# A tenth product on GpSimd in every chunk of a selective scan, and an earlier request for the rows of B

## The chip, the cores and the metric

The kernel runs on one core of a Trainium2 chip, as one program from the first load to the last store. The metric is the device time of that core in microseconds (us), the median of several executions. Below, TensorE is PE, VectorE is DVE, ScalarE is ACT, GpSimd is POOL and SyncE is SP.

## What is computed

Four layers, one after the other, each a vision block built on a selective scan over images of 64 x 64 tokens (8 images, 96 channels, doubled to 192 inside). Three layers scan in four directions, the last in one. Cut to what matters, a direction does this for every channel d and each of 16 states n:

```
delta = softplus(dts + bias)                    # per channel and token
def step(h, inp):
    u_t, d_t, b_t, c_t = inp
    dA = jnp.exp(d_t[..., None] * A[None])
    h = dA * h + (d_t * u_t)[..., None] * b_t[:, :, None, :]
    y = jnp.einsum('bkdn,bkn->bkd', h, c_t)
    return (h, y)
```

The product of delta*u (in the kernel: du) and B feeds the recurrence, and the product of h and C is summed over the 16 states. Around the scan stand projections, a depthwise convolution, a norm and a gate, which the change doesn't touch.

## The kernel before

Each layer is three stages: `expand_stage`, `scan_stage` and `merge_stage`. The change is in `scan_stage` alone. It works on chunks of 1024 tokens of a pair of images in one direction; 208 chunks in all (64 in each of the first three layers, 16 in the last). A loop body holds two chunks (`BODY_CHUNKS`), so there are 104 bodies, and all orders are written out by hand inside a body.

A chunk has three tiles of channels (`TILES`) with 16 states each: 48 **steps**. Two steps make a **unit**, so a chunk has 24 units, eight to a tile (`TILE_UNITS`), and a body 48. In this text units are counted 0 to 23 in a chunk; the tiles are units 0 to 7, 8 to 15 and 16 to 23. Four units (a quad) share one copy of delta and of du, `delta4_` (three buffers) and `du4_` (two buffers), spread over the partitions by DMA.

What happens to a unit depends on where its product du*B is made:

- In most units PE copies the rows of B over the partitions into PSUM (`slot`, L899), ACT makes the decay exp(delta*A) into `decay` (L1102), DVE multiplies du with the slot, one instruction a step (L1037), and DVE scans, one instruction a step (L1063).
- In the units named by `POOL_UNITS`, 2, 5 and 7 of each tile, nine in a chunk, POOL makes the product for both steps in one instruction of 128 x 2048 elements into `made` (L1284), from `du4_` and from rows of B that a DMA has spread into `b4_` (two buffers, `B_RING`). ACT puts the decay into the slot, and DVE only scans (L1059).

Behind the scans of every unit POOL multiplies h with C for both steps (`gate`, L1263), and PE sums over the states (`reduce`, L969). POOL also makes du = delta*u once a tile (L1276). POOL's order, in each unit v: at v = 4 of a tile the du of the next tile; then, if unit v + 2 is one of POOL's (`POOL_LEAD` is 2), its product; then the gate of v, which waits for the scans of v.

SP issues all the DMAs from one queue, in order, and waits in that queue. For each unit v, `after_gate` does this, in this order: in units 8 to 11 of each half chunk of 12, the rows of C for four units later (`load_c`, four DMAs); if v is one of POOL's units, the rows of B for the product two further on (`load_b`, four DMAs); in unit 4 of a tile the first quad of du of the next tile (`spread_du`, eight DMAs); in unit 7 its second quad; in unit 3 the first quad of delta of the next tile (`spread_delta`, eight DMAs); in unit 4 its second quad. Ahead of rows of C, rows of B, and the second quad of du, SP waits on `gated` until the gate of v is done (L807); ahead of the others it waits for `du_ready` (L814) or `delta_ready` (L820). The order in unit 4 of the last tile, where all three fall together, is thus: rows of C, du, delta.

On DVE, the first multiply of a quad waits until all eight DMAs of its du have landed (`du_in`, L1034), and both scans of a POOL unit wait for `pool_multiplied` (L1058). Each new quad of du overwrites the quad before the last.

Of the kernel before, what the change touches and what calls it, by code (L numbers as in the profile page):

```python
# [31 lines left out]
TILES = 3  # L32
# [20 lines left out]
QUADS, GROUP = 4, 32  # L53
UNITS = STEPS // 2
TILE_UNITS = UNITS // TILES
PAIRS_OF_GROUPS = UNITS // QUADS
BATCH_UNITS = UNITS // 2


POOL_UNITS, POOL_LEAD = (2, 5, 7), 2  # L60
H_RING, DECAY_RING, DELTA_RING, DU_RING, B_RING, MADE_RING = 4, 3, 3, 2, 2, 2
AHEAD, FILL_LAG, REDUCE_LAG = 2, 2, 2
FLAT = 2 * NS * CH // P
# [10 lines left out]
DU_AT, Y_STORE = 4, 1  # L74
# [523 lines left out]
def scan_stage(nc, kind, T, W, useq, neg_a, yseq, bcdram, splitdram):  # L598
# [18 lines left out]
    BU = BODY_CHUNKS * UNITS  # L617
    BODY_PAIRS = BODY_CHUNKS * PAIRS_OF_GROUPS


    on_pool = [v for v in range(BU) if v % TILE_UNITS in POOL_UNITS]
    PB = len(on_pool)
    assert PB % B_RING == 0 and PB % MADE_RING == 0 and BU % H_RING == 0 and BODY_PAIRS % DELTA_RING == 0 and BODY_PAIRS % DU_RING == 0

    def place(s):
# [7 lines left out]
    def pair_of(v):  # L633

        return v // QUADS
# [20 lines left out]
    C_BODY = 64 * 2 * BODY_CHUNKS  # L656
    B_BODY = 64 * PB // B_RING
    DELTA_BODY = 128 * BODY_PAIRS // DELTA_RING
# [8 lines left out]
    with ExitStack() as ctx:  # L667
# [52 lines left out]
        with nc.Block() as block:  # L720
            @block.sync
            def _(sp):
# [34 lines left out]
                def load_quad(dst, signal, v, base):  # L757


                    q = v // UNITS % BODY_CHUNKS  # L760
                    for j in range(QUADS):
                        row = base + NS * batch_of(v) + QUADS * (v % QUADS) + j
                        sp.dma_start(dst[GROUP * j:GROUP * j + GROUP, :],
                                     bcdram[q, row:row + 1, :].broadcast_to((GROUP, CH))).then_inc(signal, 16)

                def load_c(v):
                    load_quad(c4[v % QUADS], c_in[v % QUADS], v, 2 * NS)

                def load_b(k):
                    load_quad(b4[k % B_RING], b_in[k % B_RING], on_pool[k % PB] + BU * (k // PB), 0)  # L770

# [10 lines left out]
                def spread_delta(j):  # L782
                    spread_pair(delta4[j % DELTA_RING], delta_in[j % DELTA_RING], delta[:, 1:], j)

                def spread_du(j):
                    spread_pair(du4[j % DU_RING], du_in[j % DU_RING], du, j, 1)

                def store_y(i, C0, T_):

                    q, t = T_ // TILES, T_ % TILES  # L790
                    sp.wait_ge(sem["y_copied"], C0 * TILES + (T_ + 2))
                    here = chunk_and_direction(i, q)[0]
                    if backward(q):
                        here = here + SEQS[kind] * PAIRS * NCH
                    sp.dma_start(yseq[here, t], ybuf[:]).then_inc(sem["y_stored"], 16)

                def after_gate(i, C0, v):

                    if v % TILE_UNITS == Y_STORE and v >= TILE_UNITS:
                        store_y(i, C0, v // TILE_UNITS - 1)  # L800
                    if v >= BU:
                        return
                    n, T_ = v % TILE_UNITS, v // TILE_UNITS
                    new_c, new_b = v % BATCH_UNITS >= BATCH_UNITS - QUADS, v in on_pool
                    if new_c or new_b or n == DU_OUT_AT[1]:

                        sp.wait_ge(sem["gated"], C0 * UNITS + (v + 1 + REDUCE_LAG))  # L807
                    if new_c:
                        load_c(v + QUADS)
                    if new_b:  # L810
                        load_b(on_pool.index(v) + B_RING)
                    if n == DU_OUT_AT[0]:

                        sp.wait_ge(sem["du_ready"], C0 * TILES + (T_ + 2))  # L814
                        spread_du(2 * T_ + 2)
                    if n == DU_OUT_AT[1]:
                        spread_du(2 * T_ + 3)
                    if n == DELTA_OUT_AT[0]:

                        sp.wait_ge(sem["delta_ready"], C0 * TILES + (T_ + 2))  # L820
                        spread_delta(2 * T_ + 2)
                    if n == DELTA_OUT_AT[1]:
                        spread_delta(2 * T_ + 3)
# [36 lines left out]
                for v in range(Y_STORE + 1):  # L860
                    after_gate(0, 0, v)
                with sp.Fori(0, NC // BODY_CHUNKS) as i:
                    C0 = i * BODY_CHUNKS
                    for v in range(Y_STORE + 1, BU + Y_STORE + 1):
                        after_gate(i, C0, v)
                        if v < BU:
                            chunk_work(i, C0, v)
# [158 lines left out]
            def _(dve):  # L1026
# [13 lines left out]
                def scan(C0, body, s, g):  # L1040
# [15 lines left out]
                    if v in on_pool:  # L1056
                        p = on_pool.index(v)
                        dve.wait_ge(sem["pool_multiplied"], body * PB + (p + 1))  # L1058
                        dve.tensor_tensor_scan(out, slot[s % 2][:, order], made[p % MADE_RING][:, s % 2, order],  # L1059
# [193 lines left out]
            def _(pool):  # L1253
# [24 lines left out]
                def multiply(i, v):  # L1278

                    k = on_pool.index(v % BU) + PB * (v // BU)  # L1280
                    j = pair_of(v)
# [397 lines left out]
def build(nc, args, out, layers=(0, 1, 2, 3)):  # L1679
# [12 lines left out]
    with ExitStack() as ctx:  # L1692
# [25 lines left out]
        for n in layers:  # L1718
            kind = KINDS[n]
            count = SEQS[kind] * PAIRS * NCH  # L1720
            results = DIRS[kind] * PAIRS * NCH
            expand_stage(nc, kind, T, W[n], x_t, useq[0:count], zgate)
            scan_stage(nc, kind, T, W[n], useq[0:count], neg_a[n], yseq[0:results], bcdram, splitdram)
            merge_stage(nc, kind, T, W[n], useq[0:count], yseq[0:results], zgate, x_t, out, n == layers[-1])
# [110 lines left out]
```

## Time and profile before

| | us |
|---|---|
| median of 3 runs | 36543.74 (36541.12 to 36548.06) |
| the profiled execution | 36523.66 |
| its span | 36521.8 |
| DVE busy | 33315.6 |
| POOL busy | 31312.7 |
| PE busy | 26890.5 |
| ACT busy | 18989.0 |

The profiled execution lies 20 us below the median, and only 1.9 us lie outside its span. The span is made of four scan stages, where all of this change happens, and of the stages around them. The busy times are of the whole span, so they mix stages with different limits: a scan stage has to be read by itself. In the rows below, a row of the timeline gives the start of an instruction (or of several in a row, then with the time of all of them), its time, the engine, the line, what is written and read, the count, and in brackets the idle time of the engine before it and what ended it. Queue rows of SP (SPq) show the time that SP took to issue the DMAs, not when they landed.

### The profile page before, as it was taken

Reading aid. Unit: us, or ns where it says so; the run is one execution under the profiler, and the core shown is the slowest. Engines: PE = TensorE matmul, PEld = TensorE weight load, DVE = VectorE, ACT = ScalarE, POOL = GpSimd, SP = SyncE. Lnnn points to the kernel's source line nnn. Section 1 sums busy time; section 2 is a strip of 40 time slices with the busy share of each in tenths; the row PEclk is TensorE's granted clock in tenths of the full one; section 3 lists DMA queues with packets and bytes.
Section 4 is the critical chain, followed back from the end, with each engine's and each line's share of the span. In section 5 each row is a group of like instructions: output and inputs, shape, how many; then the busy total and the mean of one; then the engine's idle time right before and its main releaser. Section 6 shows DMA issues by size and latency. Waiting matters only on the chain. (4 is left out here: it accounts for less than half of the span.)

```text
span 36521.8 us, 335475 instructions
## 1 busy us (share of the span) xinstructions
PE 26890.5 (74%) x76784; PEld 7510.4 (21%) x76784; DVE 33315.6 (91%) x18007; ACT 18989.0 (52%) x23286; POOL 31312.7 (86%) x7984
## 2 busy tenths in 40 slices
PE   5777777777766777777777766777777777766777
PEld 2111111111122111111111112111111111112114
DVE  6999999999977999999999977999999999976993
ACT  4555555555534555555555534555555555534551
POOL 1999999999962999999999961999999999974993
PEclk7888888888878888888888878888888888877885
DMA  4666666666675666666666675666666666676665
GB/s 154 172 174 173 174 174 173 173 171 174 173 237 175 173 172 174 172 173 173 172 171 173 172 233 173 174 171 173 173 174 172 172 173 172 172 240 183 174 174 178
DMA packets 2428244, 6486.11 MB, mean 178 GB/s; under 512 B 704848, under 2 KB 849616, under 8 KB 2416336
## 3 DMA queue, kind: packets, MB, share of 16 engines
q1 hardware_dynamic: 2426576, 6471.86, 66.8%
q14 instruction: 1597, 13.08, 0.1%
q8 instruction: 71, 1.16, 0.0%
HBM read 3070.92 MB, written 764.47 MB: 105 GB/s over the span
## 5 line engine op out<-in xcount | busy, mean ns | idle before, releaser
L1263 POOL TENSOR_TENSOR h<-h,c 128x2048 f32<-128x2048 f32 x4992 | 20775.3, 4178 | 571.6 <-DVE h L1063 423.3
L1063 DVE TENSOR_TENSOR_SCAN h<-decay,state,slot 128x1024 f32<-128x1024 f32 x6240 | 14647.7, 2347 | 832.8 <-issue 44.8
L969 PE MATMUL psy<-h,t_fold 128*32 128x512 f32 x40000 | 11405.6, 749 | 0.0
L899 PE MATMUL slot<-bc,pick 96*128 96x512 bf16 x12496 | 4654.1, 461 | 7571.8 <-DVE h L1059 5930.6
L1059 DVE TENSOR_TENSOR_SCAN h<-slot,state,made 128x1024 f32<-128x1024 f32 x3744 | 8565.8, 2327 | 8.8 <-ACT slot L1102 8.8
L1284 POOL TENSOR_TENSOR made<-du,b 128x2048 f32<-128x2048 f32 x1872 | 7804.1, 4169 | 723.6 <-DMA b<-bcdram 723.6
L1102 ACT ACTIVATE decay<-delta,na 128x1024 f32<-128x1024 f32 x6248 | 7066.8, 1145 | 1706.0 <-DVE h L1063 1519.0
L1037 DVE TENSOR_TENSOR slot<-du,slot 128x1024 f32<-128x1024 f32 x6240 | 7534.5, 1207 | 281.6 <-PE slot L899 254.8
L1102 ACT ACTIVATE slot<-delta,na 128x1024 f32<-128x1024 f32 x3744 | 4177.0, 1116 | 4262.3 <-DVE h L1063 4255.1
L969 PEld LDWEIGHTS psy<-h,t_fold 128*32 128x32 f32 x40000 | 2290.1, 130 | 8286.4 <-issue 7772.2
L899 PEld LDWEIGHTS slot<-bc,pick 96*128 96x128 bf16 x12496 | 776.8, 102 | 13297.0 <-DVE h L1059 9058.9
L1276 POOL TENSOR_TENSOR du<-delta,u 128x1024 f32<-128x1024 f32 x628 | 1473.0, 2346 | 2356.1 <-ACT delta L1156 2356.1
L1110 ACT COPY state<-h 128x2 f32<-128x2 f32 x4992 | 924.1, 185 | 3934.9 <-DVE h L1063 2979.0
L917 PE MATMUL psc<-dts,wdt 32*128 32x512 f32 x2512 | 1921.1, 853 | 0.9 <-ACT dts L1190 0.9
L1654 POOL TENSOR_TENSOR ya<-ya,yb 128x1024 f32<-128x1024 f32 x360 | 997.5, 2779 | 849.8 <-DMA ub<-useq 783.8
L907 PE MATMUL psc<-u,wx 128*96 128x512 f32 x2544 | 1551.8, 728 | 6.7 <-DMA bdt<-in_bdt 6.2
L1125 ACT ACTIVATE relu<-psc,bdt 128x1024 f32<-128x1024 f32 x628 | 699.8, 1114 | 1561.9 <-PE psc L917 1561.9
L1156 ACT COPY delta<-psc 128x1024 f32<-128x1024 f32 x628 | 637.2, 1015 | 1428.5 <-PE psc L936 1428.5
L1598 DVE SCALAR_TENSOR_TENSOR total<-ub,dsum,ya 128x1024 f32<-128x1024 f32 x240 | 464.7, 1943 | 899.7 <-DMA ub<-useq 514.1
L936 PE MATMUL psc<-log,t_ident 128*128 128x512 f32 x2512 | 1220.6, 608 | 8.9 <-ACT log L1139 0.2
L936 PE MATMUL psc<-relu,t_ident 128*128 128x512 f32 x2512 | 1215.1, 607 | 9.2 <-ACT ex L1126 9.2
L936 PE MATMUL psc<-excess,t_less 128*128 128x512 f32 x2512 | 1181.9, 592 | 0.0
(111 smaller groups left out, 19226.2 us busy)
## 6 DMA issues: line engine op xcount, KB each, us to landing
delta<-delta SPq DMA_DIRECT2D x10048, 128.0 KB, 2.6
du<-du SPq DMA_DIRECT2D x10048, 128.0 KB, 2.9
b<-bcdram SPq DMA_DIRECT2D x7520, 128.0 KB, 2.9
c<-bcdram SPq DMA_DIRECT2D x6720, 128.0 KB, 2.9
u<-useq SPq DMA_DIRECT2D x212, 1536.0 KB, 6.7
yseq<-ybuf SPq DMA_DIRECT2D x624, 512.0 KB, 3.0
ya<-yseq SPq DMA_DIRECT2D x420, 512.0 KB, 4.4
yb<-yseq SPq DMA_DIRECT2D x360, 512.0 KB, 5.3
```

The lines of the kernel that those rows point to most:

```text
L899: mm = pe.matmul(slot[s % 2][:, cols], pick[:, rows_of, :], bc[q % 2][:, cols], start=True, stop=True)
L907: mm = pe.matmul(psc[0:96, HALF[a]], wx[q][:, s, :], u[q][:, s, HALF[a]], start=(s == 0), stop=(s == TILES - 1))
L917: pe.matmul(psc[:, HALF[a]], wdt[q][:, t, :], dts[q][:, HALF[a]], start=True, stop=True)\
L936: mm = pe.matmul(psc[:, HALF[a]], T["less" if term == 2 else "ident"][:, :], (relu, log, excess, ex)[term][:, HALF[a]], start=(term == 0), ...
L969: mm = pe.matmul(psy[rows, cols], T["fold"][:, :], h[v % H_RING][:, c, cols], start=(v % QUADS == 0), stop=(v % QUADS == QUADS - 1), skip_ ...
L1037: dve.tensor_tensor(slot[s % 2][:], du4[j % DU_RING][:, s % 2, 1:], slot[s % 2][:], ALU.mult)\
L1059: dve.tensor_tensor_scan(out, slot[s % 2][:, order], made[p % MADE_RING][:, s % 2, order], first, ALU.mult, ALU.add).then_inc(sem["h_ready ...
L1063: dve.tensor_tensor_scan(out, decay[s % DECAY_RING][:, order], slot[s % 2][:, order], first, ALU.mult, ALU.add).then_inc(sem["h_ready"], 1)
L1102: act.activation(dst[:], delta4[j % DELTA_RING][:, s % 2, :], ACT.Exp, scale=na[q][:, k:k + 1])\
L1263: pool.tensor_tensor(both[:, :, 0:CH], both[:, :, 1:], c4[g][:, order].unsqueeze(1).broadcast_to((P, 2, CH)), ALU.mult)\
L1276: pool.tensor_tensor(du[:], delta[:, 1:], u[q][:, t, :], ALU.mult).then_inc(sem["du_ready"], 1)
L1284: pool.tensor_tensor(made[k % MADE_RING][:], du4[j % DU_RING][:, :, 1:], b4[k % B_RING][:].unsqueeze(1).broadcast_to((P, 2, CH)), ALU.mult)\
```

## The change

`POOL_UNITS` gets an entry for each of the three tiles: in the third tile of a chunk POOL makes the products of units 1, 3, 5 and 7 in place of 2, 5 and 7 (in the chunk: 17, 19, 21, 23 in place of 18, 21, 23). That is ten products a chunk, and DVE has 14 units with multiplies in place of 15. And SP asks for rows of B not at the place of the unit v whose product used the buffer, but at v - 2, where that product is made (but at unit 2 at the earliest, in the body's first tile). So in its queue SP meets B in units 3 and 5 of a tile where it met it in 5 and 7, and in the last tile in 1, 3, 5 and, for the next chunk's first product, at its unit 0.

```
-POOL_UNITS, POOL_LEAD = (2, 5, 7), 2
+POOL_UNITS, POOL_LEAD = ((2, 5, 7), (2, 5, 7), (1, 3, 5, 7)), 2
...
-    on_pool = [v for v in range(BU) if v % TILE_UNITS in POOL_UNITS]
+    on_pool = [v for v in range(BU) if v % TILE_UNITS in POOL_UNITS[v // TILE_UNITS % TILES]]
     PB = len(on_pool)
+
+    product_made = [max(v - POOL_LEAD, Y_STORE + 1) for v in on_pool]
...
-                    new_c, new_b = v % BATCH_UNITS >= BATCH_UNITS - QUADS, v in on_pool
+                    new_c, new_b = v % BATCH_UNITS >= BATCH_UNITS - QUADS, v in product_made
                     if new_c or new_b or n == DU_OUT_AT[1]:
+
 
                         sp.wait_ge(sem["gated"], C0 * UNITS + (v + 1 + REDUCE_LAG))
...
                     if new_b:
-                        load_b(on_pool.index(v) + B_RING)
+                        load_b(product_made.index(v) + B_RING)
```

POOL's instructions in the third tile of the body's first chunk, from the product made ahead of the gate of unit 15 on. `made` is a product, `h` with `c4` a gate (h3 is unit 15, h0 unit 16, h1 unit 17, h2 unit 18). Before:

```order
L1263 TENSOR_TENSOR h2_0<-h2_0,c4_2_0 128x2x1024
L1257 REGISTER_ALU
L1263 TENSOR_TENSOR h3_0<-h3_0,c4_3_0 128x2x1024
L1282 REGISTER_ALU
L1283 REGISTER_ALU
L1284 TENSOR_TENSOR made0_0<-du4_0_0,b4_0_0 128x2048
L1257 REGISTER_ALU
L1263 TENSOR_TENSOR h0_0<-h0_0,c4_0_0 128x2x1024
```

Now:

```order
L1266 TENSOR_TENSOR h2_0<-h2_0,c4_2_0 128x2x1024
L1285 REGISTER_ALU
L1286 REGISTER_ALU
L1287 TENSOR_TENSOR made0_0<-du4_0_0,b4_0_0 128x2048
L1260 REGISTER_ALU
L1266 TENSOR_TENSOR h3_0<-h3_0,c4_3_0 128x2x1024
L1260 REGISTER_ALU
L1266 TENSOR_TENSOR h0_0<-h0_0,c4_0_0 128x2x1024
L1287 TENSOR_TENSOR made1_0<-du4_0_0,b4_1_0 128x2048
L1260 REGISTER_ALU
```

The product of the tile's first POOL unit (17, not 18) now stands ahead of the gate of 15, and a further one (of 19) ahead of the gate of 17.

SP's queue in the third tile, units 18 to 20 before (from the wait for the gate of unit 18 to the second quad of delta):

```order
L807 REGISTER_ALU
L763 DMA b4_0_0<-bcdram 32x1024 [waits gated]
L763 DMA b4_0_0<-bcdram 32x1024 x3
L820 REGISTER_ALU
L778 DMA delta4_0_0<-delta_0 32x1024 [waits delta_ready]
L778 DMA delta4_0_0<-delta_0 32x1024 x7
L807 REGISTER_ALU
L763 DMA c4_0_0<-bcdram 32x1024 [waits gated]
L763 DMA c4_0_0<-bcdram 32x1024 x3
L778 DMA du4_0_0<-du_0 32x1024 [waits du_ready]
L778 DMA du4_0_0<-du_0 32x1024 x7
L778 DMA delta4_1_0<-delta_0 32x1024 x8
```

Now, units 19 and 20 (the wait for the gate of unit 19 is the first row):

```order
L810 REGISTER_ALU
L765 DMA b4_0_0<-bcdram 32x1024 [waits gated]
L765 DMA b4_0_0<-bcdram 32x1024 x3
L823 REGISTER_ALU
L780 DMA delta4_0_0<-delta_0 32x1024 [waits delta_ready]
L780 DMA delta4_0_0<-delta_0 32x1024 x7
L810 REGISTER_ALU
L765 DMA c4_0_0<-bcdram 32x1024 [waits gated]
L765 DMA c4_0_0<-bcdram 32x1024 x3
L780 DMA du4_0_0<-du_0 32x1024 [waits du_ready]
L780 DMA du4_0_0<-du_0 32x1024 x7
L780 DMA delta4_1_0<-delta_0 32x1024 x8
```

The rows read alike, but the `gated` of the rows of B just ahead of the delta is that of unit 18 before, and of unit 19 now.

## Rows read from the trace of the kernel before

**Rows 1.** The page: the costliest groups of the scan, whole program

```profile
L1263 POOL TENSOR_TENSOR h<-h,c 128x2048 f32<-128x2048 f32 x4992 | 20775.3, 4178 | 571.6 <-DVE h L1063 423.3
L1063 DVE TENSOR_TENSOR_SCAN h<-decay,state,slot 128x1024 f32<-128x1024 f32 x6240 | 14647.7, 2347 | 832.8 <-issue 44.8
...
L1059 DVE TENSOR_TENSOR_SCAN h<-slot,state,made 128x1024 f32<-128x1024 f32 x3744 | 8565.8, 2327 | 8.8 <-ACT slot L1102 8.8
L1284 POOL TENSOR_TENSOR made<-du,b 128x2048 f32<-128x2048 f32 x1872 | 7804.1, 4169 | 723.6 <-DMA b<-bcdram 723.6
...
L1037 DVE TENSOR_TENSOR slot<-du,slot 128x1024 f32<-128x1024 f32 x6240 | 7534.5, 1207 | 281.6 <-PE slot L899 254.8
```

**Rows 2.** Busy time by stretch: the four scan stages

```profile
core 0: us, PE busy (x) PEld busy (x) DVE busy (x) ACT busy (x) POOL busy (x), PEclk, DMA share, GB/s
814.00:10321.00 9507.00, 7244.08 (x20998) 1858.67 (x20994) 9243.23 (x4985) 5289.80 (x6596) 9166.82 (x2302) 0.83 0.68 173
11747.00:21285.00 9538.00, 7262.22 (x20996) 1862.62 (x20992) 9243.49 (x4985) 5290.32 (x6596) 9167.54 (x2302) 0.82 0.68 172
```

**Rows 3.** By stretch: one body; and unit 10 of its second chunk to the next body

```profile
5855.33:6151.53 296.20, 224.31 (x658) 57.92 (x656) 289.12 (x156) 165.40 (x206) 286.26 (x73) 0.83 0.69 173
6070.37:6150.20 79.83, 56.71 (x173) 14.30 (x172) 77.92 (x43) 42.94 (x54) 78.20 (x20) 0.82 0.63 159
```

**Rows 4.** Timeline of DVE: units 10, 18, start of 19, 23, next unit 0

```profile
6065.75 4.62 DVE L1059 TENSOR_TENSOR_SCAN h<-slot,state,made 128x1024 f32<-128x1024 f32 x2
...
6115.14 4.57 DVE L1059 TENSOR_TENSOR_SCAN h<-slot,state,made 128x1024 f32<-128x1024 f32 x2
6119.63 1.21 DVE L1037 TENSOR_TENSOR slot<-du,slot 128x1024 f32<-128x1024 f32 x1
...
6126.81 1.21 DVE L1037 TENSOR_TENSOR slot<-du,slot 128x1024 f32<-128x1024 f32 x1
...
6145.65 4.57 DVE L1059 TENSOR_TENSOR_SCAN h<-slot,state,made 128x1024 f32<-128x1024 f32 x2
6150.20 1.23 DVE L1037 TENSOR_TENSOR slot<-du,slot 128x1024 f32<-128x1024 f32 x1
```

**Rows 5.** Timeline of POOL from the gate of unit 10 to the next body's first product

```profile
6070.44 4.18 POOL L1263 TENSOR_TENSOR h<-h,c 128x2048 f32<-128x2048 f32 x1 [0.36 <-DVE h L1059]
6074.57 4.17 POOL L1284 TENSOR_TENSOR made<-du,b 128x2048 f32<-128x2048 f32 x1
6078.70 4.18 POOL L1263 TENSOR_TENSOR h<-h,c 128x2048 f32<-128x2048 f32 x1
6082.84 2.33 POOL L1276 TENSOR_TENSOR du<-delta,u 128x1024 f32<-128x1024 f32 x1
6085.14 4.16 POOL L1263 TENSOR_TENSOR h<-h,c 128x2048 f32<-128x2048 f32 x1
...
6115.31 4.18 POOL L1263 TENSOR_TENSOR h<-h,c 128x2048 f32<-128x2048 f32 x1 [1.26 <-DVE h L1063]
6119.79 4.18 POOL L1263 TENSOR_TENSOR h<-h,c 128x2048 f32<-128x2048 f32 x1 [0.30 <-DVE h L1059]
...
6158.30 4.17 POOL L1284 TENSOR_TENSOR made<-du,b 128x2048 f32<-128x2048 f32 x1 [3.13 <-DMA b<-bcdram]
```

**Rows 6.** Timeline of SP's queue in units 11 to 13 and 18 to 21

```profile
6094.77 5.25 SPq L778 DMA_DIRECT2D delta<-delta  x8
6100.14 1.90 SPq L763 DMA_DIRECT2D b<-bcdram  x4
...
6123.99 1.70 SPq L763 DMA_DIRECT2D b<-bcdram  x4
6130.35 4.96 SPq L778 DMA_DIRECT2D delta<-delta  x8
6138.69 1.71 SPq L763 DMA_DIRECT2D c<-bcdram  x4
6140.44 4.97 SPq L778 DMA_DIRECT2D du<-du  x8
6145.45 5.11 SPq L778 DMA_DIRECT2D delta<-delta  x8
```

**Rows 7.** DMAs of du: the eight of that group; then all 96 of about a body

```profile
L778 SPq DMA_DIRECT2D du<-du x8: 513/592/602, 6140.4 to 6144.8; - x8
...
DMA to landing us min/median/max: 2.8/3.0/3.2
```

```profile
L778 SPq DMA_DIRECT2D du<-du x96: 512/592/1144, 6011.9 to 6293.3; - x96
...
DMA to landing us min/median/max: 2.4/3.0/4.9
```

**Rows 8.** DVE's scans by line: scan stages of the first, second and third layer

```profile
L1063 DVE TENSOR_TENSOR_SCAN h<-decay,state,slot 128x1024 f32<-128x1024 f32 x1917 | 4499.9, 2347 | 238.5 <-ACT state L1207 13.1
...
L1063 DVE TENSOR_TENSOR_SCAN h<-decay,state,slot 128x1024 f32<-128x1024 f32 x1917 | 4499.9, 2347 | 270.8 <-issue 44.8 <-ACT decay L1102 3.1
...
L1063 DVE TENSOR_TENSOR_SCAN h<-decay,state,slot 128x1024 f32<-128x1024 f32 x1917 | 4499.9, 2347 | 260.3 <-DVE slot L1037 22.9 <-ACT state L1207 12.5 <-ACT decay L1102 6.9
```

**Rows 9.** Timeline of DVE where a body begins, in the second layer

```profile
14119.40 1.23 DVE L1037 TENSOR_TENSOR slot<-du,slot 128x1024 f32<-128x1024 f32 x1 [0.78 <-issue]
14121.84 2.35 DVE L1063 TENSOR_TENSOR_SCAN h<-decay,state,slot 128x1024 f32<-128x1024 f32 x1 [1.21 <-issue]
```

## Prediction

> **What bounds the kernel now.** First I read the costliest groups of the page [rows 1], then the busy time of each scan stage by itself [rows 2], then one body and one stretch of it [rows 3], and only then the timelines. The reader should see in [rows 2] that a stage of 9507 us has DVE busy for 9243 us and POOL for 9167: over 96% both. The rest of DVE's time is mostly the gap of about 0.1 us between two instructions, so in the scan DVE practically never waits. Its rhythm stands in the timeline [rows 4]: a unit whose product POOL makes takes 4.49 us (6115.14 to 6119.63), a unit with its own multiplies 7.18 us (6119.63 to 6126.81). A body of 18 and 30 such units is 18 x 4.49 + 30 x 7.18 = 296.2 us, and the body that I read takes 296.20 [rows 3]. POOL, in contrast, still waits a little: for scans (1.26, 0.36 and 0.30 us [rows 5]), and for rows of B (3.13 us in [rows 5], 723.6 us in the whole program [rows 1]). So DVE sets the time, and POOL is some 2% behind it.
>
> **Part one: the earlier request for B.** It takes away the wait of 723.6 us [rows 1]. I cost it at nothing by itself: the wait is POOL's, at the first product of a chunk, and DVE runs through those same units without a wait (a body lasts exactly the sum of its units [rows 3]). Shifted alone it would give back POOL time that nobody needs. Its price is in SP's queue: in the last tile the request now stands in unit 19, behind a wait for that unit's gate and ahead of the delta and du spreads of the next tile.
>
> **Part two: the tenth product.** DVE loses one unit's two multiplies: 7.18 - 4.49 = 2.69 us a chunk, 208 x 2.69 = 560 us if nothing else came late. POOL gains one product of 4.13 us (6074.57 to 6078.70, start to start [rows 5]). Per chunk DVE would need 10 x 4.49 + 14 x 7.18 = 145.4 us and POOL 24 + 10 operations of 4.13 and three du of 2.30 (6082.84 to 6085.14), 147.3 us, against 148.1 us of DVE now. So of 560 us at most 208 x (148.1 - 147.3) = 166 us can be had, and only if POOL never waits.
>
> It will wait, because the extra load is all in the last tile. I take one stretch of the timeline [rows 3 to 5]: in unit 10 POOL has caught up (its gate starts 0.07 us behind the scans, 6065.75 + 4.62 = 6070.37 against 6070.44), and in the new order nothing ahead of that point is heavier, so it will have caught up there again. The measure is the time from the end of the scans of unit 10 to the first multiply of the next chunk: now 6150.20 - 6070.37 = 79.83 us, all of it DVE's own work. In the new order three chains run over the same stretch:
>
> - DVE itself: 79.83 - 2.69 = 77.1 us.
> - POOL's last product (unit 23), which DVE needs. From the gate of unit 10 on POOL has 11 gates, 6 products and 2 du ahead of its end: 0.07 + 17 x 4.13 + 2 x 2.30 + 0.05 (an operation lasts about 0.05 us beyond the next one's start) = 74.9 us. With 0.08 us to wake DVE and 4.57 us for the two scans of unit 23 [rows 4] the next chunk starts at 79.6 us. So the saving on DVE is used up by a wait for that product, to within 79.83 - 79.6 = 0.2 us.
> - The du of the next chunk's first quad, through SP. The gate of unit 19 ends after 10 gates, 5 products and 1 du: 0.07 + 15 x 4.13 + 2.30 + 0.05 = 64.4 us. Only then may SP issue B (1.70 us, at 6123.99 in [rows 6]), the delta (4.96), C (1.90, as a group of four took directly behind delta at 6100.14) and du. With the small gaps between them (0.03, 0.10, 0.12 and 0.04) the du group begins at 73.2 us. Its last DMA is issued 4.4 us later (6140.4 to 6144.8 [rows 7]) and lands after 2.8 us (the lowest of that group; the median is 3.0): 80.4 us, and with 0.07 us to wake DVE **80.5 us**. The wait for gate 20 ahead of C is no limit, since that gate ends at 64.4 + 2.30 + 4.13 = 70.8 us and SP arrives at 71.2.
>
> Before, du was early: its last DMA was issued at 6144.8 and landed at about 6147.6, 2.6 us ahead of the multiply. Now both its cover (the slack) and the 2.69 us of DVE work that stood over it are gone. The third chain ends last, so a chunk lasts 80.5 - 79.8 = 0.7 us longer than now, not 2.69 less: 208 x 0.67 = +139 us.
>
> **What is hidden in it.** DVE pauses where a new body begins: in the second layer before the first multiply and the first scan, with nothing that the profile could name [rows 9], 44.8 us in its 32 bodies [rows 8]. In the first and third layer the rows name 13.1, 22.9 and 12.5 us more. Together that is 93 us. A wait for du in front of the first multiply runs at the same time as such a pause. I take 74 us of it, about four fifths, as hidden under the new wait (bounds: 0 and 93). Sum: +139 - 74 = **+65 us**. In the profiled execution's terms that is 36523.66 + 65 = 36589, and on the median 36543.74 + 65 = 36609.
>
> The other tiles are no trouble: in units 3 and 11 POOL is only 1 to 2 us behind, so du is issued some 5 us earlier relative to DVE. PE and ACT have work for 76% and 56% of a body [rows 3] and lose the fills of two units a body. Operations of POOL and DVE keep their times: the products take 4.17 us while DVE is busy all the time, so more of them add no new kind of neighbour.
>
> **What the Trainium skill says to it.** A product takes 4.17 us [rows 5], the two multiplies that it replaces 2 x 1.207 = 2.41 us [rows 1]. The Trainium skill, "GPSIMD Engine Reference", sections 3.1 and 4.1, speaks against the change: two-input elementwise work belongs on VectorE, and a float32 tensor_tensor of 2048 elements takes 4497 ns on GpSimd. With that figure for the six products the second chain would end 6 x 0.33 = 2.0 us later, an estimate of about +1.7 us a chunk; the trace has the duration, and decides for 4.17.
>
> The landing of a du DMA takes 2.8 to 3.2 us [rows 7]. The Trainium skill, "DMA: Bandwidth & Descriptors", section "Anatomy of one DMA", gives 2.0 us plus the bytes at 436 GB/s (for the path through GpSimd): for 128 KB an estimate of 2.3 us. By that du would land 0.5 us earlier and the sum would be 0.5 x 208 = 104 us lower; the rows of the trace don't support it.
>
> **The rivals.**
>
> - **Du lands in time, the product alone sets the pace.** It happens if SP gets through its four groups 0.9 us faster. A chunk takes 79.6 us over the stretch: -0.28 x 208 = -58 us, 36486. For it: the groups have been seen a little shorter. Against: it takes the lowest figures for all four at once.
> - **POOL never waits.** If POOL comes into each chunk late enough to be busy throughout, its 147.3 us set the period: -166 us, 36378. Against it: the first 11 units of a chunk hold four POOL units in the new order as before, and there POOL catches up today.
> - **The du chain is longer: slower.** Landings of up to 4.9 us are seen [rows 7]. The queue now carries four groups back to back. If the last du lands 1 us later than I take, that is another +208 us (36817); at 4.9 us, 2.1 us later, +437 us (37046). It decides from a landing of 2.84 us on that the kernel is slower by over 0.2%. For it: after long runs of C and B groups landings grow. Against: delta groups, issued at a slower pace, stand between them, and the du group that follows a C group [rows 6] still landed in 2.8 to 3.2 us.
> - **The change doesn't do what it says:** a wait for B stays, because SP comes late to the earlier place. It would cost POOL time only where DVE doesn't wait for it, and leave the sum as it is.
>
> **How the numbers follow.** The forecast (new wait for du of about 0.9 us a chunk behind a wait of about 2.4 us for the last product) has a chance of 0.60, with a range of its own of 36500 to 36720; du in time 0.13; POOL saturated, or another gain, 0.07; the longer chain 0.20. The predicted time is 36609. The range of 36470 to 36760 leaves out the saturated case and most of the longer chain. About 0.2% (73 us) is what a measurement of this kernel can tell from no change. The forecast lies just inside that: of its 0.60 I give 0.37 to no change, 0.21 to slower and 0.02 to faster; of the case with du in time 0.10 to no change and 0.03 to faster; of the longer chain 0.19 to slower. That makes 0.12 faster, 0.47 same, 0.41 slower, rounded with the rest.
>
> **What would show it.** Multiplies on DVE fall from 6240 to 5824 and products rise from 1872 to 2080. The wait of POOL for B vanishes. DVE's scans L1059 should show waits on POOL's product, about 208 x 2.4 = 500 us, at unit 23 of each chunk; the multiplies should show waits on the du DMA, 0.5 to 1.2 us each, 208 times. POOL's busy time rises by 208 x 4.17 = 867 us and it still waits about 0.4 us in unit 10. The prediction is wrong if the first multiply of a chunk doesn't wait for du, if POOL's gate of unit 10 starts well behind its scans, or if a wait stands in another tile.

## The result and the profile after

| | us |
|---|---|
| changed kernel, median of 20 runs | 36597.0 (36589.04 to 36611.18) |
| kernel before, on the same chip, median of 20 runs | 36544.93 (36526.74 to 36556.71) |
| ratio | 1.0015 (95% interval 1.0008 to 1.0021) |
| profiled execution's span, before and after | 36521.8 and 36600.3 |

The change makes the kernel 0.15% slower: +52 us by the medians. The forecast was +65 us, 36609. One execution of the kernel before and one of `du_and_last_product_first` ran in a slower state of the chip (46085 and 47182 us, at a granted clock of 0.62 and 0.56), and no ratio in this text uses them.

The page of the changed kernel, first the busy times, then the groups that answer to [rows 1] (L1040 was L1037, L1062 was L1059, L1066 was L1063, L1266 was L1263, L1287 was L1284):

```profile
PE 27123.1 (74%) x75952; PEld 7532.9 (21%) x75952; DVE 32861.6 (90%) x17591; ACT 18974.0 (52%) x23286; POOL 32158.8 (88%) x8192
...
L1266 POOL TENSOR_TENSOR h<-h,c 128x2048 f32<-128x2048 f32 x4992 | 20774.8, 4179 | 404.6 <-DVE h L1066 309.3
L1066 DVE TENSOR_TENSOR_SCAN h<-decay,state,slot 128x1024 f32<-128x1024 f32 x5824 | 13670.9, 2347 | 728.5 <-DVE slot L1040 30.5
...
L1062 DVE TENSOR_TENSOR_SCAN h<-slot,state,made 128x1024 f32<-128x1024 f32 x4160 | 9519.4, 2329 | 393.8 <-POOL made L1287 308.9
...
L1287 POOL TENSOR_TENSOR made<-du,b 128x2048 f32<-128x2048 f32 x2080 | 8679.1, 4173 | 123.1 <-DMA b<-bcdram 123.1
L1040 DVE TENSOR_TENSOR slot<-du,slot 128x1024 f32<-128x1024 f32 x5824 | 7035.6, 1208 | 520.9 <-PE slot L902 323.3
```

The work has moved as the diff says: 416 multiplies went to POOL as 208 products. DVE is busy for 454 us less (33315.6 before), POOL for 846 us more (31312.7 before), and the mean times of the instructions are within 0.1% of those before. POOL's wait for B fell from 723.6 us [rows 1] to 123.1, which is four waits of up to 30.9 us, one at the start of each scan stage. But two waits have appeared on DVE, which ran through the scan almost without one: 308.9 us for POOL's product, and one for du, which the view of groups by line shows in full (columns as on the page, with every releaser):

```profile
L1062 DVE TENSOR_TENSOR_SCAN h<-slot,state,made 128x1024 f32<-128x1024 f32 x4160 | 9519.4, 2329 | 393.8 <-POOL made L1287 308.9 <-ACT slot L1105 83.2 <-issue 1.0
L1040 DVE TENSOR_TENSOR slot<-du,slot 128x1024 f32<-128x1024 f32 x5824 | 7035.6, 1208 | 520.9 <-PE slot L902 323.3 <-DMA du<-du 197.6
```

The scan stages by themselves, to be laid beside [rows 2] (busy times of PE, PEld, DVE, ACT, POOL; granted clock; DMA): the first is now 9556 us and the second 9533, where they were 9507 and 9538. DVE fell to 9104 busy us, POOL rose to 9427: POOL is now the fuller of the two.

```profile
814.00:10370.00 9556.00, 7314.31 (x20745) 1868.00 (x20744) 9103.85 (x4859) 5288.65 (x6597) 9426.95 (x2367) 0.83 0.69 176
11797.00:21330.00 9533.00, 7286.38 (x20740) 1861.76 (x20734) 9100.49 (x4857) 5283.83 (x6595) 9424.32 (x2366) 0.83 0.69 176
```

Now one stretch of the kind that the prediction measured: from the end of the scans of unit 10 to the first multiply of the next chunk. Timeline of DVE (start, time, engine, line, what, count, idle time before it): unit 10, unit 19, unit 23, and the next unit 0.

```profile
6092.02 4.62 DVE L1062 TENSOR_TENSOR_SCAN h<-slot,state,made 128x1024 f32<-128x1024 f32 x2
...
6146.83 4.59 DVE L1062 TENSOR_TENSOR_SCAN h<-slot,state,made 128x1024 f32<-128x1024 f32 x2 [0.85 <-ACT slot L1105]
...
6171.61 4.59 DVE L1062 TENSOR_TENSOR_SCAN h<-slot,state,made 128x1024 f32<-128x1024 f32 x2 [1.35 <-POOL made L1287]
6177.75 1.23 DVE L1040 TENSOR_TENSOR slot<-du,slot 128x1024 f32<-128x1024 f32 x1 [1.54 <-DMA du<-du]
```

POOL over the same place: the gate of unit 10, which waits a last time; then the gate of unit 19, the du of the tile, the gate of 20, and the product of unit 23.

```profile
6096.72 4.18 POOL L1266 TENSOR_TENSOR h<-h,c 128x2048 f32<-128x2048 f32 x1 [0.35 <-DVE h L1062]
...
6156.82 4.20 POOL L1266 TENSOR_TENSOR h<-h,c 128x2048 f32<-128x2048 f32 x1
6160.94 2.37 POOL L1279 TENSOR_TENSOR du<-delta,u 128x1024 f32<-128x1024 f32 x1
6163.25 4.20 POOL L1266 TENSOR_TENSOR h<-h,c 128x2048 f32<-128x2048 f32 x1
6167.38 4.20 POOL L1287 TENSOR_TENSOR made<-du,b 128x2048 f32<-128x2048 f32 x1
```

And SP's queue (time taken to issue the group). The first row joins two groups of four, with the wait for a gate between them; the second of them goes out as soon as the gate of unit 19 has ended, at 6161.02.

```profile
6148.65 14.09 SPq L765 DMA_DIRECT2D b<-bcdram  x8
6162.85 4.97 SPq L780 DMA_DIRECT2D delta<-delta  x8
6167.93 1.91 SPq L765 DMA_DIRECT2D c<-bcdram  x4
6169.89 4.96 SPq L780 DMA_DIRECT2D du<-du  x8
6174.88 5.42 SPq L780 DMA_DIRECT2D delta<-delta  x8
```

The du buffer in the same stretch (durations of the issues, first and last start; who waited; from issue to landing): its last DMA is issued at 6174.2 and lands after up to 3.5 us, at 6177.7, and at 6177.75 DVE goes on.

```profile
L780 SPq DMA_DIRECT2D du<-du x8: 513/591/594, 6169.9 to 6174.2; - x8
...
  DVE slot L1040: 1.5, 1
...
DMA to landing us min/median/max: 3.0/3.1/3.5
```

So the reader sees one queue with B, delta, C and du back to back behind one gate of POOL, and DVE at its end. The stretch of this chunk is 6177.75 - 6096.64 = 81.1 us. Over all chunks of the trace its mean is 80.37 us for the first chunk of a body and 80.74 for the second; in the kernel before these were 79.80 and 80.16.

### The profile page after: what moved, and what is told of

Read it like the earlier page. It is cut to its first block and busy times, and to the rows that moved or that the text cites. A ratio compares the mean times of both kernels' runs of the same rounds, so it can differ in the third digit from the quotient of the medians.

```text
span 36600.3 us, 334539 instructions
## 1 busy us (share of the span) xinstructions
PE 27123.1 (74%) x75952; PEld 7532.9 (21%) x75952; DVE 32861.6 (90%) x17591; ACT 18974.0 (52%) x23286; POOL 32158.8 (88%) x8192
## 5 line engine op out<-in xcount | busy, mean ns | idle before, releaser
L1266 POOL TENSOR_TENSOR h<-h,c 128x2048 f32<-128x2048 f32 x4992 | 20774.8, 4179 | 404.6 <-DVE h L1066 309.3
L1066 DVE TENSOR_TENSOR_SCAN h<-decay,state,slot 128x1024 f32<-128x1024 f32 x5824 | 13670.9, 2347 | 728.5 <-DVE slot L1040 30.5
L972 PE MATMUL psy<-h,t_fold 128*32 128x512 f32 x40000 | 11860.4, 735 | 57.6 <-POOL h L1266 57.6
L1062 DVE TENSOR_TENSOR_SCAN h<-slot,state,made 128x1024 f32<-128x1024 f32 x4160 | 9519.4, 2329 | 393.8 <-POOL made L1287 308.9
L902 PE MATMUL slot<-bc,pick 96*128 96x512 bf16 x11664 | 4376.5, 465 | 7327.6 <-DVE h L1062 5878.0
L1287 POOL TENSOR_TENSOR made<-du,b 128x2048 f32<-128x2048 f32 x2080 | 8679.1, 4173 | 123.1 <-DMA b<-bcdram 123.1
L1040 DVE TENSOR_TENSOR slot<-du,slot 128x1024 f32<-128x1024 f32 x5824 | 7035.6, 1208 | 520.9 <-PE slot L902 323.3
L1105 ACT ACTIVATE slot<-delta,na 128x1024 f32<-128x1024 f32 x4160 | 4639.9, 1115 | 5480.7 <-DVE h L1066 5475.1
L1105 ACT ACTIVATE decay<-delta,na 128x1024 f32<-128x1024 f32 x5832 | 6595.0, 1145 | 1553.9 <-DVE h L1066 1044.0
```

The lines of the kernel that those rows point to most:

```text
L902: mm = pe.matmul(slot[s % 2][:, cols], pick[:, rows_of, :], bc[q % 2][:, cols], start=True, stop=True)
L972: mm = pe.matmul(psy[rows, cols], T["fold"][:, :], h[v % H_RING][:, c, cols], start=(v % QUADS == 0), stop=(v % QUADS == QUADS - 1), skip_ ...
L1040: dve.tensor_tensor(slot[s % 2][:], du4[j % DU_RING][:, s % 2, 1:], slot[s % 2][:], ALU.mult)\
L1066: dve.tensor_tensor_scan(out, decay[s % DECAY_RING][:, order], slot[s % 2][:, order], first, ALU.mult, ALU.add).then_inc(sem["h_ready"], 1)
L1105: act.activation(dst[:], delta4[j % DELTA_RING][:, s % 2, :], ACT.Exp, scale=na[q][:, k:k + 1])\
L1266: pool.tensor_tensor(both[:, :, 0:CH], both[:, :, 1:], c4[g][:, order].unsqueeze(1).broadcast_to((P, 2, CH)), ALU.mult)\
```

## The experiments

In every run below, the stretch runs from the end of the scans of unit 10 to the next chunk's first multiply, and is a mean over the whole trace; where two figures stand, they are those of the first and of the second chunk of a body. My theory was that of the prediction: three chains run over that stretch, DVE's own work (shortest), POOL's last product, and the du of the next chunk through SP's queue (longest, it sets the time). Its rivals: (a) the wait for the product is what costs, and the du is only late because everything is; (b) the earlier request for B does the harm in SP's queue; (c) POOL is simply full, whatever the order. Each experiment is given against the changed kernel. The kernel before ran beside them, on other chips than the changed one above, and took 36523.6 us with the first four, 36533.4 us with the next four, and 36531.7 us with the last two. So kernels of different groups are compared by what each gains or loses to the kernel before beside it; the changed kernel loses 52 us.

### The two parts apart

Nine products, with the earlier request for B (`early_b_nine`):

```
-POOL_UNITS, POOL_LEAD = ((2, 5, 7), (2, 5, 7), (1, 3, 5, 7)), 2
+POOL_UNITS, POOL_LEAD = ((2, 5, 7), (2, 5, 7), (2, 5, 7)), 2
```

> The earlier request for B alone, with nine products a chunk as before. Theory (a chunk of the changed kernel is as long as it is because the du of the next chunk comes late through SP's queue, behind a last product that is late too): with nine products POOL's gates are early again, so the time is that of the kernel before, 36545 us within 25, though POOL's wait for B (723.6 us before) is gone. Rival (the request itself, with its wait for the gate of unit 19 ahead of delta and du, costs the time): 36597 us as in the changed kernel, and waits for du on VectorE.

Ten products, with B asked for at the old place (`late_b_ten`):

```
-    product_made = [max(v - POOL_LEAD, Y_STORE + 1) for v in on_pool]
+    product_made = list(on_pool)
```

> Ten products, rows of B asked for at the old place. Theory: POOL's products in the last tile then stand two units apart while B is asked for one gate (4.13 us) ahead, and the request for unit 17 stands behind the du and delta groups of unit 12; POOL waits some us for B several times a chunk, and since POOL has no time to spare this lands on the time: 37100 to 38000 us, POOL waiting for B over 1000 us in total. Rival (the early request gives nothing, since the wait it removes was off the path): within 60 us of 36597.

Measured: 36522.47 us for the first, ratio 0.9999 to the kernel before (0.9990 to 1.0008). No time is won or lost, although POOL's wait for B is gone there too. The view of waits (engine and line, what was waited for: us in total, times, longest) shows where it went: POOL now waits for DVE in its place, 934.4 us against 423.3 [rows 1].

```profile
POOL h L1266 <- DVE h L1066: 934.4, 655, 9.7
```

The second took 37651.42 us, ratio 1.0308 (1.0289 to 1.0328). Its waits:

```profile
POOL made L1287 <- DMA b<-bcdram: 1482.0, 579, 32.5
DVE h L1062 <- POOL made L1287: 1233.5, 854, 2.9
DVE slot L1040 <- DMA du<-du: 213.2, 198, 1.9
```

POOL waits twice as long for B as before, and with ten products it has no time to make up for it, so DVE waits too. To the kernel before that is a loss of 1128 us, where the changed kernel loses 52. The early request for B is worth nothing with nine products and about 1076 us with ten. Rival (b) falls in so far as the request by itself costs nothing, and taking it away makes ten products worse. It is still a link of the du chain: with ten products its four DMAs stand between the late gate of unit 19 and the delta. No run moves that one request alone out of du's way.

### Du ahead of the rest in SP's queue, and behind more of it

`du_first`: in unit 4 of a tile the first quad of du, with its own wait for `du_ready`, goes ahead of the wait for the gate and of the rows of C and B. The work is the same.

```
                     new_c, new_b = v % BATCH_UNITS >= BATCH_UNITS - QUADS, v in product_made
+                    if n == DU_OUT_AT[0]:
+                        sp.wait_ge(sem["du_ready"], C0 * TILES + (T_ + 2))
+                        spread_du(2 * T_ + 2)
                     if new_c or new_b or n == DU_OUT_AT[1]:
...
-                    if n == DU_OUT_AT[0]:
-                        sp.wait_ge(sem["du_ready"], C0 * TILES + (T_ + 2))
-                        spread_du(2 * T_ + 2)
```

> The changed kernel with the first quad of du put ahead of the rows of C in unit 4 of a tile. Theory: the du chain is 1.9 us shorter and is in time; then the last product alone ends last, 79.6 us after the scans of unit 10 in place of 80.3 to 80.7, which is 0.7 to 1.1 us a chunk: 36390 to 36460 us, faster than before; no wait for du on VectorE, and the wait for the last product stays at about 1.5 us. Rival (the last product sets the pace already, and the wait for du is only what is left of it): 36597 within 25. Second rival (POOL and VectorE slow one another): 36597 as well, with longer operations.

`du_behind_delta`: in the last tile the second quad of delta goes ahead of that du, eight DMAs more in front of it.

```
+                    if n == DELTA_OUT_AT[1] and T_ % TILES == 2:
+                        spread_delta(2 * T_ + 3)
                     if n == DU_OUT_AT[0]:
...
-                    if n == DELTA_OUT_AT[1]:
+                    if n == DELTA_OUT_AT[1] and T_ % TILES != 2:
```

> The changed kernel with the second quad of delta put ahead of the first quad of du, in the last tile only. Theory: the du chain gets 5.1 us longer and lands on the time one to one, 208 x 5.1 = 1060 us: 37600 to 37700 us, and the wait for du at the first multiply of a chunk becomes about 6 us. Rival (the last product sets the pace): at most the part beyond the present wait, about 4.2 us a chunk, if it is late at all. Where the mechanism is wrong altogether: 36597.

Measured: `du_first` 36390.1 us, ratio 0.9963 (0.9949 to 0.9977), so 133 us faster than the kernel before and, with the 52 us that the changed kernel loses, about 186 us better than that one. The stretch is 79.48 us (79.46 in the second chunk), where the prediction's chain over the product ends at 79.6. Nobody waits for du now, and DVE still waits for the product as before. Groups by line:

```profile
L1059 DVE TENSOR_TENSOR_SCAN h<-slot,state,made 128x1024 f32<-128x1024 f32 x4160 | 9516.6, 2328 | 392.9 <-POOL made L1284 300.1 <-ACT slot L1102 83.9 <-ACT decay L1102 7.0
L1037 DVE TENSOR_TENSOR slot<-du,slot 128x1024 f32<-128x1024 f32 x5824 | 7028.6, 1207 | 324.6 <-PE slot L899 324.3 <-issue 0.2
```

`du_behind_delta` took 37586.28 us, ratio 1.0290 (1.0271 to 1.0310). The stretch is 85.44 and 85.57 us: 4.95 us longer than in the changed kernel, which is the time of the eight DMAs (4.96 to 5.42 us in the rows above). Its waits, beside those for the product, which stay:

```profile
DVE slot L1042 <- DMA du<-du: 1215.3, 204, 7.2
DVE h L1064 <- POOL made L1289: 297.5, 202, 2.4
```

A queue entry ahead of the du costs its issue time, one to one, in every chunk: the du is the last link. Rival (a) falls here: the same 300 us of waiting for the product stand in a kernel some 186 us faster than the changed one and in one some 1010 us slower.

### POOL's last product earlier

`last_product_first`: POOL makes the product of unit 23 ahead of the gate of unit 20, one gate earlier.

```
-                        if v + POOL_LEAD in on_pool:
+                        if v % UNITS == 20:
+                            multiply(i, v + 3)
+                        if v + POOL_LEAD in on_pool and v % UNITS != 21:
```

> The changed kernel with POOL's last product of a chunk (unit 23) made ahead of the gate of unit 20, not behind it. It ends 4.1 us earlier, the gate of unit 20 4.1 us later. Theory (SP's chain to du ends last): the rows of C wait for that gate and du stands behind them, so du lands at 74.9 + 1.9 + 4.4 + 2.8 = about 84.1 us after the scans of unit 10 in place of 80.5: +3.6 x 208 = +750 us on the changed kernel, about 37330 us. Rival (the last product ends last): 0.3 to 2 us a chunk less, 36200 to 36540 us.

`du_and_last_product_first` has this and the edit of `du_first`.

> Both moves: du ahead of C, and the last product ahead of the gate of unit 20. Theory: du then hangs on the gate of unit 19 alone (78.5 us), the product is in time, and what is left is POOL's own work, 34 x 4.13 + 3 x 2.30 = 147.3 us a chunk: some 0.36 us a chunk below du_first, 75 us, so about 36315 us; POOL has no idle time in unit 10 any more. Rival (POOL cannot be kept busy throughout, since a chunk's first units still make it wait): 36390 as du_first.

Measured: `last_product_first` 37282.27 us, ratio 1.0204 (1.0187 to 1.0222). DVE no longer waits for the product at all, and the kernel loses 749 us to the kernel before, some 700 us more than the changed one. The queue of SP says why:

```profile
6120.70 4.97 SPq L780 DMA_DIRECT2D delta<-delta  x8
6129.43 1.71 SPq L765 DMA_DIRECT2D c<-bcdram  x4
6131.18 4.97 SPq L780 DMA_DIRECT2D du<-du  x8
```

The rows of C wait for the gate of unit 20, which now comes one product later. SP stands still from 6125.67 to 6129.43, and the du behind it lands later by that: the stretch is 83.73 and 84.15 us, 3.4 us longer. DVE waits for du 1234.7 us. A wait removed from the one chain went into the longer one. With du out of that wait's way, the same edit gives 36369.51 us, ratio 0.9954 (0.9941 to 0.9966); 36315 was expected. Its stretch is still 79.45 us, although du and product both come in time. The view of waits names a chain that I had not counted, PE's fill of the slot for the first multiply, 645.6 us where it was 323.3:

```profile
DVE slot L1037 <- PE slot L899: 645.6, 282, 64.8
```

In PE's program the sum of unit 20 stands ahead of that fill. The sum needs the gate of unit 20, which has moved behind the product. `fill_before_reduce` below tests this.

### Half of the last product

`half_last_product`: POOL makes only half of the tokens of the product of unit 23; the other half is left out, so this part of the scan's input isn't computed. `half_last_product_du_first` has the edit of `du_first` as well.

```
-                    pool.tensor_tensor(made[k % MADE_RING][:], du4[j % DU_RING][:, :, 1:],
-                                       b4[k % B_RING][:].unsqueeze(1).broadcast_to((P, 2, CH)), ALU.mult)\
+                    w = CH // 2 if v % UNITS == 23 else CH
+                    pool.tensor_tensor(made[k % MADE_RING][:, :, 0:w], du4[j % DU_RING][:, :, 1:1 + w],
+                                       b4[k % B_RING][:, 0:w].unsqueeze(1).broadcast_to((P, 2, w)), ALU.mult)\
```

> The changed kernel with the last product of a chunk (unit 23) made over half its width: half of that product is left out. POOL's instruction falls from 4.17 to about 2.1 us. Theory (du through SP ends last, behind the gate of unit 19, which stands ahead of this product): the wait for the product goes, the wait for du grows by as much, and the time stays, 36580 us within 40. Rival (the last product ends last): up to 1.5 us a chunk less, 36270 us.

> The same half product (half of the product of unit 23 is left out), with du ahead of the rows of C. Theory: now the product is what ends last, so the same 2.07 us count, until du ends last again at 78.5 us in place of 79.6: -1.1 x 208 = -230 us on du_first, about 36160 us. Rival (neither chain matters, the gain of du_first came from elsewhere): 36390.

| us, and against the kernel before | whole last product | half of it |
|---|---|---|
| du as in the change | 36597.0, +52 | 36609.32, +76 |
| du first | 36390.1, -133 | 36205.25, -328 |

The ratios to the kernel before are 1.0021 (1.0012 to 1.0030) and 0.9911 (0.9896 to 0.9925) in the right-hand column. With du late, 2 us less work of POOL a chunk gain nothing: the time that DVE doesn't wait for the product it waits for du, 570.1 us in place of 197.6, and the stretch is 80.38 and 81.02 us. With du first the same saving is worth 195 us (230 were expected), and the stretch falls to 78.6; there DVE waits for du again, 140.1 us in all, so the du chain is last once more. From the page of `half_last_product`, and its groups by form:

```profile
L1040 DVE TENSOR_TENSOR slot<-du,slot 128x1024 f32<-128x1024 f32 x5824 | 7033.7, 1208 | 874.7 <-DMA du<-du 570.1
```

```profile
L1288 POOL TENSOR_TENSOR made<-du,b 128x1024 f32<-128x1024 f32 x208 | 455.8, 2191 | 0.0
```

This pair is the plainest proof of the order of the chains: the du is last, the product next. It also speaks against rival (c). What settles that one is that the same ten whole products take 36597.0 us in the changed kernel, 36390.1 in `du_first` and 36291.62 in the first version below.

### Two more versions that beat both kernels

`fill_before_reduce` takes `du_and_last_product_first` and lets PE make the sum of unit 20 one step later, behind the fill that the next chunk's first multiply needs. All work is done.

```
-                        if s % 2 == 1:
-                            reduce(C0, s // 2 - REDUCE_LAG)
+                        if s % 2 == 1 and s % STEPS != 45 or s % STEPS == 46:
+                            reduce(C0, (s - 1) // 2 - REDUCE_LAG)
```

> The kernel with du and the last product first, whose first multiply of a chunk waited 1.5 us on TensorE's fill of the slot. There TensorE first sums unit 20 (which waits for that unit's gate, now 4.1 us later) and then fills the slot of the next chunk's step 0. Here the sum of unit 20 stands behind that fill. Theory (this place in TensorE's order is the third chain that ends last): the wait goes, du sets the pace at 78.5 us in place of 79.45, and POOL's own 147.3 us a chunk are the floor: 0.6 to 0.9 us a chunk less, about 36220 us (36180 to 36290). Rival (POOL is saturated already, and the wait on the fill is only where that shows): 36370 as without the move.

`tenth_in_second_tile` leaves the last tile and its queue as in `early_b_nine` and puts the tenth product into the second tile. All work is done.

```
-POOL_UNITS, POOL_LEAD = ((2, 5, 7), (2, 5, 7), (1, 3, 5, 7)), 2
+POOL_UNITS, POOL_LEAD = ((2, 5, 7), (0, 2, 4, 7), (2, 5, 7)), 2
```

> Ten products a chunk and the early request for B, with nothing moved in SP's queue, but the tile with four products is the second one (units 0, 2, 4 and 7 of it), not the third. Theory: the three chains are the same, but in the second tile no rows of C stand ahead of du behind a late gate at the tile's start; VectorE waits some 0.7 us at three products in a row, about 2.2 us a chunk, and not for du, so a chunk takes about 0.8 us less than in the changed kernel: about 36430 us (36380 to 36500), faster than before by 0.1 to 0.4%. Rival (any tenth product costs as much as it saves, since POOL has too little time): 36580 to 36600.

Measured: `fill_before_reduce` 36291.62 us, ratio **0.9933** (0.9920 to 0.9947), the fastest complete kernel of the study. The stretch is 78.66 and 78.76 us. The wait for the fill is back at 303.4 us, and what is left is small and spread over three engines:

```profile
DVE slot L1037 <- PE slot L899: 303.4, 46, 64.5
DVE slot L1037 <- DMA du<-du: 157.3, 188, 2.8
DVE h L1059 <- ACT slot L1102: 91.6, 139, 0.9
```

It missed its expected 36220 by 72 us, and the upper end of its range by 2. Groups by line have 87.0 us at L1063 that the changed kernel doesn't have, a wait for PE's sum: the first scan of the next chunk writes the buffer (`h`, four in a ring) that the sum of unit 20, now made late, still reads. And POOL's gates wait for DVE 122 us in all (91.3 and 30.8 in the view of waits), where it was 402 in the changed kernel. A body is 295.25 us in the mean, 147.6 a chunk, against the prediction's 147.3 us of POOL's own work, so in this order POOL has next to no room left.

```profile
L1063 DVE TENSOR_TENSOR_SCAN h<-decay,state,slot 128x1024 f32<-128x1024 f32 x5824 | 13669.5, 2347 | 810.1 <-PE psy L969 87.0 <-DVE slot L1037 30.8 <-ACT state L1207 29.2
```

`tenth_in_second_tile` took 36454.83 us, ratio 0.9979 (0.9970 to 0.9988), against 36430 expected. With the last tile's queue left alone it wins 77 us: DVE waits for du only 0.8 us in all, and only products are late, those of units 8, 10 and 12, by 0.9, 0.6 and 0.6 us in the mean:

```profile
DVE h L1062 <- POOL made L1287: 434.5, 622, 1.1
DVE slot L1040 <- PE slot L902: 255.5, 6, 64.8
```

## Why the prediction was right, point by point

- **What bounds the kernel before.** Right. Taking 600 us of waits from POOL (`early_b_nine`) changed nothing; POOL waited for DVE in their place.
- **The earlier B costs and gives nothing by itself.** Right with nine products (0.9999). What the prediction didn't say is that the tenth product depends on it: about 1076 us.
- **DVE's own chain, 77.1 us.** Nearly. The chunk shown has 81.11 us with 0.85 + 1.35 + 1.54 us of waits, so 77.4 without. The 0.85 was not foreseen: at unit 19 DVE waits for ACT's slot, 134 times and 83.2 us in all. At unit 18 it waits 50 times for PE's fill, 61.8 us, nearly all that this wait has grown by (323.3 us for 254.8 [rows 1]).
- **The product's chain, 79.6 us.** Right. In the chunk shown the product of unit 23 ends at 6171.58, 74.94 us after the scans of unit 10, where the sum had 74.9; two scans later it is 79.56. `du_first` takes the longer chain away, and the stretch is 79.48.
- **The du's chain, 80.5 us.** Right in place and size: 80.37 and 80.74. Link by link in the chunk shown: the gate of 19 ends at 64.38 us (64.4 in the sum), du begins at 73.25 (73.2). The last landing took about 3.5 us there, where the sum has 2.8: this one chunk is 81.1. Over all chunks the last landing takes 2.87 us in the mean (2.37 to 3.90), close to the 2.8 of the sum. The Trainium skill ("DMA: Bandwidth & Descriptors", "Anatomy of one DMA") gives a fit for the path through GpSimd, by which the landing would be an estimate of 2.3 us. These DMAs are SP's, and the trace disagrees with 3.0 to 3.5 us, the same side as [rows 7].
- **Products of 4.17 us, with more of them.** Right: 4173 ns for 2080 of them, against 4169. In `fill_before_reduce` it is 4186. The Trainium skill's 4497 ns ("GPSIMD Engine Reference", section 3.1) is again above the trace, and its advice to keep such work on VectorE decides nothing here: a tenth product is a loss in the changed kernel's order and a gain in others (0.9979 in `tenth_in_second_tile`, 0.9933 in `fill_before_reduce`).
- **The new waits.** The wait for du: 197.6 us in 208 chunks, 0.95 us each, inside the 0.5 to 1.2 forecast. The wait for the product was mis-sized: 308.9 us, 1.5 a chunk, not 2.4. That forecast was the product's 79.6 less DVE's own 77.1, and DVE's chain is what was short. What DVE waits earlier, at units 18 and 19 for PE and ACT (0.70 us a chunk), it doesn't wait for the product. Most of the rest is the one chunk taken as the base: 79.83, where the mean over all chunks is 79.98. The sum didn't hang on this wait, since the du ends later.
- **The sum.** 208 chunks longer by 0.57 and 0.58 us make 120 us (139 forecast, mostly since its base of 79.83 was 0.15 below the mean). The bodies grew by only 0.54 us each in the mean (297.66 to 298.20), 56 us in 104 bodies, so 64 us of the 120 were made up elsewhere in the body (74 forecast). Most of it is in the second layer, whose bodies got shorter, 298.14 to 297.75 us: the pauses before the first scan [rows 8, 9] that the profile couldn't name are gone. The row of the second layer alone has none left:

```profile
L1066 DVE TENSOR_TENSOR_SCAN h<-decay,state,slot 128x1024 f32<-128x1024 f32 x1789 | 4199.4, 2347 | 210.9
```

The reason that the prediction gave for this term isn't shown. It let the wait for du run at the same time as these pauses, but the 44.8 us stand before the first scan, one multiply behind that wait, and they are gone in `du_first` too, where nothing waits for du. So the size of the term is in part luck; and since both terms came out lower than forecast (120 for 139, 64 for 74), their errors partly cancelled in the sum.

The profiled executions differ by 78.5 us. About 21 of the 22 us beyond the bodies lie outside the four scan stages, where the change does nothing, and I can't name their cause; the medians differ by 52.

- **The rivals.** POOL saturated did not come about, since POOL caught up at unit 10 as said (its gate 0.08 us behind the scans, after 0.35 us of idle time). The longer chain did not come about either: landings do grow behind a long run of C and B (the du group issued from 6160.7 in the kernel before, behind 20 such DMAs, landed after up to 4.0 us), but the du that counts stands directly behind four. No wait for B stayed beyond the four at the stages' starts. Du in time is what `du_first` makes of it, and there the rival had a gain of 58 us (0.28 a chunk, where the prediction's own 79.83 - 79.58 is 0.25) and the run shows 133. Two things are in the difference. By the means over all chunks the stretch falls from 79.80 and 80.16 to 79.48 and 79.46, 0.51 us a chunk or 106 us, where I had taken one chunk of 79.83 and 0.28; and in the second layer, with its unnamed pauses, a body falls by 2.56 us (298.14 to 295.58), more than twice what it does in any other layer.

## What to carry to other kernels

When work is moved from the engine that bounds a loop to one that is a few per cent behind, follow the chains over the stretch where the receiving engine is latest, including the DMA queue that waits for that engine: here one chunk is 0.5 us shorter where the product ends last (`du_first`) and 0.6 us longer where the queue does, and that decided between a gain of 0.4% and a loss of 0.15%. In a queue that issues in order, put the transfer with the nearest reader ahead of the wait that it doesn't need; that cost nothing and gave some 186 us. And a wait that the profile names on the bounding engine isn't yet a cost: halving the work behind the wait for the product gave nothing until the wait behind it was gone.

## What the runs showed of the hardware

- The pauses before the first scan of a body in the second layer, which no event explains (44.8 us in all [rows 8]), are still there in `early_b_nine` (36.0 us) and gone in the changed kernel and in `du_first`. In `tenth_in_second_tile` they are gone as well, but there DVE stops 96 times before a multiply for nothing that the profile names, 56.4 us in all, where it is 24.5 us in `early_b_nine`. What causes or removes such pauses stays open.
- A product of POOL on half the tokens takes 2191 ns where the whole takes 4173: twice the half is 209 ns more than the whole, so little of it is fixed.
- SP needs about 0.43 us to issue one DMA of rows of B or C (1.70 us for four), and 0.62 us for one of du or delta (4.96 us for eight), although each moves 128 KB. With four groups behind one gate, issue alone took from 6161.0 to 6174.8, and the landing of about 3 us came on top.
